# A neighbour-max graph kernel: three base rounds instead of four, rows in blocks, late rounds at two widths

## The reference

```python
h = maximum(layernorm(x), 0)
vals, idx = top_k(where(adj != 0, -arange(N), -inf), 25)
agg = max over the kept neighbours of h[idx]        # (with 0 where 25 or fewer)
out = x + relu(concat([h, agg], -1) @ W + b)
```

## Time and profile before

| | |
|---|---|
| median of 3 runs | 662.07 us (659.44 to 663.03) |
| the profiled execution's own time | 664.44 us |
| its span, first to last instruction | 661.5 us |
| TensorE busy / VectorE busy | 596.5 / 597.0 us |
| ScalarE busy / GpSimd busy | 401.7 / 96.3 us |
| DMA queue q1 | 55.6% of 16 engines |
| mean granted TensorE clock | 0.980 |

### The profile page before, as it was taken

The page is one execution under the profiler, slowest core; times in us unless marked ns, Lnnn a source line. Parts: engine busy times, 40 slices in busy tenths (PEclk is TensorE's granted clock), DMA queues, the critical chain, the costliest instruction groups (busy, mean ns, idle before and its releaser), DMA issues.

```text
span 661.5 us, 9819 instructions
## 1 busy us (share of the span) xinstructions
PE 596.5 (90%) x2800; PEld 249.8 (38%) x2800; DVE 597.0 (90%) x731; ACT 401.7 (61%) x552; POOL 96.3 (15%) x142
## 2 busy tenths in 40 slices
PE   4678979899998999999998999999998999999886
PEld 2213333343434334343433444343433434343423
DVE  4965969999998999999999999999999999999996
ACT  3346837767486756858577666858477664846210
POOL 1400005000060002400060002400060000500000
PEclk9968989999999999999999999999999999999998
DMA  8745875858259593567558485567558262231100
GB/s 342 233 116 204 322 190 205 218 158 274 55 210 231 184 241 121 193 166 250 166 206 237 146 248 174 190 160 266 149 211 237 99 184 64 91 149 34 47 16 16
DMA packets 99437, 115.79 MB, mean 175 GB/s; under 512 B 66003, under 2 KB 85718, under 8 KB 94934
## 3 DMA queue, kind: packets, MB, share of 16 engines
q1 hardware_dynamic: 98262, 114.46, 55.6%
q10 hardware_dynamic: 1152, 1.05, 0.5%
HBM read 58.85 MB, written 20.97 MB: 121 GB/s over the span
## 4 chain that ended last, share of the span: by engine, by line
PE 53%; DVE 23%; issue 10%; DMA 5%; ACT 5%; SPq 2%; DVEq 1%; ACTq 0%
PE picked L639 17%; PE picked L640 15%; PE ring L568 9%; DVE best L827 8%; DVE late_hot L839 5%; DVE best L833 4%; PE final L666 2%; PE side L597 2%; PE side L596 2%; PE final L670 2%; DMA late_skew<-late 2%; DVE hot L814 2%; PE final L620 1%; DMA kept<-chosen 1%; ACT late L480 1%
## 5 line engine op out<-in xcount | busy, mean ns | idle before, releaser
L827 DVE TENSOR_TENSOR best<-picked,best 128x1024 f32<-128x1024 f32 x224 | 270.0, 1218 | 23.3 <-PE picked L640 21.9
L639 PE MATMUL picked<-hot,h_hi 128*128 128x512 f16 x512 | 196.6, 384 | 11.9 <-DVE best L833 6.8
L640 PE MATMUL picked<-hot,h_lo 128*128 128x512 f16 x512 | 195.9, 383 | 0.0
L639 PE MATMUL picked<-late_hot,hi_skew 128*128 128x512 f16 x344 | 130.5, 379 | 19.3 <-DVE late_hot L839 10.9
L640 PE MATMUL picked<-late_hot,lo_skew 128*128 128x512 f16 x344 | 130.3, 379 | 0.0
L833 DVE TENSOR_TENSOR best<-picked,best 128x1024 f32<-128x1024 f32 x86 | 105.0, 1221 | 15.4 <-PE picked L640 14.9
L467 ACT ACTIVATE late_rank<-ring,late_bias 128x512 bf16<-128x512 f32 x128 | 81.9, 686 | 60.4 <-PE ring L568 60.1
L467 ACT ACTIVATE rank<-ring,late_bias 128x512 bf16<-128x512 f32 x120 | 82.5, 688 | 49.0 <-PE ring L568 48.8
L475 ACT ACTIVATE chosen<-side,bias_cut 128x512 bf16<-128x512 f32 x120 | 81.9, 682 | 16.7 <-PE side L597 16.7
L498 ACT COPY best<-picked 128x1024 f32<-128x1024 f32 x32 | 32.4, 1013 | 85.3 <-PE picked L640 85.3
L639 PEld LDWEIGHTS picked<-hot,h_hi 128*128 128x128 f16 x512 | 50.4, 99 | 86.0 <-DVE best L827 15.5
(11 more groups left out here) (89 smaller groups left out, 490.9 us busy)
## 6 DMA issues: line engine op xcount, KB each, us to landing
adj_in<-in_adj_dram SPq DMA_DIRECT2D x15, 2048.0 KB, 8.6
picks<-kept SPq DMA_DIRECT2D x15, 1024.0 KB, 5.0
kept<-chosen SPq DMA_DIRECT2D x112, 128.0 KB, 3.1
late_skew<-late SPq DMA_DIRECT2D x32, 192.0 KB, 4.0
x_in<-in_x_dram SPq DMA_DIRECT2D x8, 512.0 KB, 6.3
late_skew<-late SPq DMA_DIRECT2D x16, 256.0 KB, 4.8
late_skew<-late SPq DMA_DIRECT2D x32, 128.0 KB, 3.6
xres<-in_x_dram SPq DMA_DIRECT2D x16, 256.0 KB, 2.7
```

The source lines that it names most:

```text
L639: nc.tensor.matmul(dst, hi[:, slot, k, :], onehot, start=start, stop=False)
L640: return nc.tensor.matmul(dst, lo[:, slot, k, :], onehot, start=False, stop=stop)
L827: nc.vector.tensor_tensor(best[:, half, s, :, :], picked[s][:, :, :], best[:, half, s, :, :], ALU.max).then_inc(picked_read, 1)
```

## The change

BASE becomes 3: a group has 12 uses, uses 4 to 11 in its own step. Placing is spread over uses 6 to 11 and ranks over 5 to 10, 8 blocks over 6 uses each. Six blocks of late ranks, not four, stand between use 1 and `project`. Rows are laid out by blocks: row q*128 + p of a group is at column q*128 + p, where before it was row p*4 + q; the adjacency, residual and output DMAs have 4 runs per partition where they had one. The count is reduced separately for columns 0 to 255 and 256 to 511, GpSimd works out two loop counts, and the late rounds run n+1 times at 512 columns, then m times (m at least 1) at 256 columns. The gain of the next batch's normalisation is computed at the end of an even group, where it was done in use 5 of an odd group.

```diff
-BASE = 4
+BASE = 3
+    WIDE = ROWS // 2
-    SELECT_WITH, RANK_WITH = spread_over(7, 14), spread_over(6, 13)
-    LATE_EARLY, LATE_WITH, COUNT_WITH, COUNT_USE, LATE_HOT_USES = 4, {4: (4, 5), 5: (6, 7)}, (6, 7), 8, (13, 14)
-    LATE_USES, HIGH_USE, TURN_USE = {14: (0, 1), 15: (2, 3)}, 10, 15
-    STATS_USES, MOMENTS_USE, GAIN_USE = (9, 10), 12, 5
+    SELECT_WITH, RANK_WITH = spread_over(6, 11), spread_over(5, 10)
+    LATE_EARLY, LATE_WITH, COUNT_WITH, COUNT_USE, LATE_HOT_USES = 6, {4: (6, 7)}, (5, 6), 7, (8, 9)
+    LATE_USES, HIGH_USE, TURN_USE = {11: (0, 1, 2, 3)}, 8, 11
+    STATS_USES, MOMENTS_USE = (7, 8), 9
-    adj_v = adj.rearrange("b (h p q) j -> (b h) p (q j)", p=P, q=Q)
+    adj_v = adj.rearrange("b (h q p) j -> (b h) p q j", p=P, q=Q)
...
-                nc.gpsimd.tensor_scalar(late_half[:, :], late_other[:, 0:1], late_other[:, 1:2], late_other[:, 2:3], ALU.max,
-                                        ALU.max).then_inc(late_halved, 1)
...
+                for i in range(2):
+                    nc.gpsimd.tensor_scalar(late_half[:, i:i + 1], late_other[:, 0, i:i + 1], late_other[:, 1, i:i + 1], late_other[:, 2, i:i + 1],
+                                            ALU.max, ALU.max).then_inc(late_halved, 1)
+                nc.gpsimd.tensor_scalar(late_full[:, 1:2], late_half[:, 1:2], late_other[:, 3, 1:2], None, ALU.max).then_inc(late_joined, 1)
+                nc.gpsimd.tensor_scalar(late_rounds[0:1, s, 1:2], late_full[:, 1:2], 1.0, None, ALU.max).then_inc(rounds_known, 1)
+                nc.gpsimd.tensor_scalar(late_full[:, 0:1], late_half[:, 0:1], late_other[:, 3, 0:1], late_full[:, 1:2], ALU.max,
+                                        ALU.subtract).then_inc(rest_known, 1)
+                nc.gpsimd.tensor_scalar(late_rounds[0:1, s, 0:1], late_full[:, 0:1], 1.0, None, ALU.max).then_inc(rounds_known, 1)
...
+                n = pe.value_load(late_rounds[0:1, u % 2, 1:2], min_val=1, max_val=NEIGHBOURS)
+                m = pe.value_load(late_rounds[0:1, u % 2, 0:1], min_val=1, max_val=NEIGHBOURS)
                 with pe.Fori(0, n) as r:
-                    late_round(g, done, r, slot)
+                    late_round(g, done, r, slot, ROWS)
                 pe.reg_add(rounds_done, rounds_done, n)
                 done = pe.snap(rounds_done)
-                late_round(g, done, 0, slot)
+                late_round(g, done, 0, slot, ROWS)
                 pe.reg_add(rounds_done, rounds_done, 1)
+                done = pe.snap(rounds_done)
+                with pe.Fori(0, m) as r:
+                    late_round(g, done, r, slot, WIDE)
...
-                    late_ranks(g + 1, at + LATE_AT, 0)
-                    late_ranks(g + 1, at + LATE_AT, 1)
-                    pick_pair(g + 1, 2, next_slot)
-                    late_ranks(g + 1, at + LATE_AT, 2)
-                    pick_pair(g + 1, 3, next_slot)
-                    late_ranks(g + 1, at + LATE_AT, 3)
+                    for k in (0, 1):
+                        late_ranks(g + 1, at + LATE_AT, k)
+                    for use in (2, 3):
+                        pick_pair(g + 1, use, next_slot)
+                        for k in (2 * use - 2, 2 * use - 1):
+                            late_ranks(g + 1, at + LATE_AT, k)
...
                 for i in range(2):
-                    take_late(s, i, done, 0)
+                    take_late(s, i, done, 0, ROWS)
+                    make_late_hot(i, numbers[:, bass.ds(n + 2, 1)], WIDE)
                 dve.reg_add(rounds_done, rounds_done, 1)
+                done = dve.snap(rounds_done)
+                with dve.Fori(0, m) as r:
+                    for i in range(2):
+                        take_late(s, i, done, r, WIDE)
+                        make_late_hot(i, numbers[:, bass.ds(n + r + 3, 1)], WIDE)
```

More of the change, by code:

```diff
@@ L67, in build @@
     TURNED = 16 * Q
-    assert C == P and K == 8 and PER_BATCH == 2 and BASE == 4
+    assert C == P and K == 8 and PER_BATCH == 2 and BASE == 3
     LANDED = 16 * K
     OUT_OF = 64.0
-    adj_v = adj.rearrange("b (h p q) j -> (b h) p (q j)", p=P, q=Q)
-    xres_v = x.rearrange("b (h p q) c -> (b h) p (q c)", p=P, q=Q)
-    out_v = out.rearrange("b (h p q) c -> (b h) p (q c)", p=P, q=Q)
+    adj_v = adj.rearrange("b (h q p) j -> (b h) p q j", p=P, q=Q)
+    xres_v = x.rearrange("b (h q p) c -> (b h) p q c", p=P, q=Q)
+    out_v = out.rearrange("b (h q p) c -> (b h) p q c", p=P, q=Q)
     x_v = x.rearrange("b (p k) c -> b p (k c)", k=K)
@@ L125, in build @@
         late_rank = sb("late_rank", [P, K, ROWS], BF16)
[L126 to L129, removed]
+        late_most = sb("late_most", [P, 2], F32)
+        late_other = sb("late_other", [1, CHAINS, 2], F32)
+        late_half = sb("late_half", [1, 2], F32)
+        late_full = sb("late_full", [1, 2], F32)
+        late_rounds = sb("late_rounds", [P, 2, 2], I32)
         hot = sb("hot", [P, 3, K, ROWS], F16)
@@ L367, in _ @@
             nc.gpsimd.memset(eye32[:, :], 1.0).then_inc(basics_made, 1)
-            nc.gpsimd.iota(numbers_i[:, :], pattern=[[1, 32]], base=0, channel_multiplier=0).then_inc(basics_made, 1)
+            nc.gpsimd.iota(numbers_i[:, :], pattern=[[1, 64]], base=0, channel_multiplier=0).then_inc(basics_made, 1)
             nc.gpsimd.iota(late_bias_i[:, :], pattern=[[0, CHAINS], [P, LINK]], base=1, channel_multiplier=1).then_inc(basics_made, 1)
@@ L419, in fold_count @@
                 for c in range(CHAINS):
-                    nc.gpsimd.tensor_scalar(late_other[:, c:c + 1], late_most[c * PART:c * PART + 1, :], LINK * P / 2 - 1, 1.0, ALU.add,
+                    nc.gpsimd.tensor_scalar(late_other[:, c, :], late_most[c * PART:c * PART + 1, :], LINK * P / 2 - 1, 1.0, ALU.add,
                                             ALU.max).then_inc(late_folded, 1)
@@ L672, in project, with late_round @@
                 last.then_inc(final_written, 1)
-            def late_round(g, done, r, slot):
+            def late_round(g, done, r, slot, width):
                 for s in range(2):
                     pe.wait_ge(picked_read, (g + 1) * READ - 1 + s)
-                    pe.wait_ge(late_hot_made[s], done + r + 1)
+                    pe.wait_ge(late_hot_made[s], done + (r + (g + 1)))
                     pe.wait_ge(late_read[s], done + r + 1)
@@ L682, in late_round @@
                             k = s * HALF + j * LINK + i
-                            last = pick(picked[s][:, j, :], hi_skew, lo_skew, k, late_hot[:, k, :], slot, i == 0, i == LINK - 1)
+                            last = pick(picked[s][:, j, 0:width], hi_skew, lo_skew, k, late_hot[:, k, 0:width], slot, i == 0,
+                                        i == LINK - 1)
                     last.then_inc(late_written[s], 1)
@@ L828, in take_pair, with take_late, make_late_hot @@
                                         ALU.max).then_inc(picked_read, 1)
-            def take_late(s, i, done, r):
+            def take_late(s, i, done, r, width):
                 dve.wait_ge(late_written[i], done + r + 1)
-                nc.vector.tensor_tensor(best[:, s, i, :, :], picked[i][:, :, :], best[:, s, i, :, :],
+                nc.vector.tensor_tensor(best[:, s, i, :, 0:width], picked[i][:, :, 0:width], best[:, s, i, :, 0:width],
                                         ALU.max).then_inc(late_read[i], 1)
-            def make_late_hot(i, which):
+            def make_late_hot(i, which, width):
                 part = slice(i * HALF, (i + 1) * HALF)
-                nc.vector.tensor_scalar(late_hot[:, part, :], late_rank[:, part, :], which, None,
+                nc.vector.tensor_scalar(late_hot[:, part, 0:width], late_rank[:, part, 0:width], which, None,
                                         ALU.is_equal).then_inc(late_hot_made[i], 1)
@@ L923, in step @@
                     take_pair(g, use, s)
-                    if use == 5:
-                        make_hot(BASE, s)
-                    if use == GAIN_USE and more and u % PER_BATCH == PER_BATCH - 1:
-                        make_gain(batch_of(it, u + 1))
                     if use == HIGH_USE and more and u % PER_BATCH == PER_BATCH - 1:
@@ L933, in step @@
                         dve.wait_ge(ring_read, at + REST_AT + K)
-                        make_late_hot(LATE_HOT_USES.index(use), numbers[:, 1:2])
+                        make_late_hot(LATE_HOT_USES.index(use), numbers[:, 1:2], ROWS)
                     if use in STATS_USES and ahead:
@@ L968, in step @@
                     take_pair(g + 1, 3, 1 - s)
+                if ahead:
+                    make_gain(batch_of(it, u) + 1)
                 finish_group(g, s, 16 * (it * (UNROLL // 2) + u // 2 + 1))
```

53 lines of the change are left out of this document (33 added, 20 removed).

## The result

The changed kernel takes 718.42 us (median of 4 runs, 716.17 to 720.21), the kernel before 661.59 us; the ratio is 1.0857, 95% interval 1.0817 to 1.0898. Slower, as forecast, but the loss is 57 us where 34.5 were forecast, and 718.4 lies just above the range's end of 718. The profiled span is 718.0 us against 661.5.

A forecast was written before the change was run, and what follows sets the result against it. TensorE's beat was taken to bound the base part, a loop of take, late_hot and 8 matmuls the late part. Base -39, late rounds +58.5 and work behind them +15 made +34.5 on 662.07: near 697 us, range 672 to 718.

The forecast's parts named there:

- Base part: Use 4 to first late take: odd groups save 2.8 us, even 1.15, the last two 5.7 each; 39 us less.
- GpSimd's ten operations: Ten tiny operations in place of six, between use 7's count and the late rounds: covered, costing nothing; uncovered 1 to 2 us a group.
- The placing chain: Placing k waits for ScalarE's chosen k-1, 1.38 us a block; TensorE waits 3.0 us a group, mainly at uses 6 and 9.
- Rival 1: Placing waits in the base part don't bite, so it gains 83 us, not 39: 653 us, faster; chance 0.07 (fully).
- The late part: Three more full rounds at 3.86 us and 21 half rounds, 46.9 us: 58.5 us more in sum.
- Rival 3: Half-width late rounds cost nearly a full one: +34 us, 731 us; chance 0.05.
- rival 5: The row split fails and rows from 256 on need as many late rounds: 66 full ones, 727 us; chance 0.01.
- Behind the late rounds: Two more late-rank blocks, three matmuls, between use 3 and project: 1.0 us in 15 groups, 15 us more.
- Rival 2: TensorE's clock falls twice a group at use 6's wait and half-round gaps: adds 20 to 35 us, 725 us; chance 0.08.
- Rival 4: The skew comes late, each odd group waiting 1 us or more for late_skew: +10, 707 us; chance 0.07.
- The range: Whole kernel, 672 to 718 us; lower end from half the placing waits gone and half rounds at their lower bound.
- the walk through its program: TensorE's in-order base part from use 4 to use 11: 58 matmuls, two counts and 3.0 us of waits, ending at 16.36 us.

The follow-up runs named there:

- before_two_reads: The kernel before, with TensorE reading its count twice: 664.97 us, ratio 1.0046.
- read_m_later: The changed kernel, with TensorE's read of the second count m moved from in front of the full-width rounds to behind them: 706.03 us, ratio 1.0672.
- third_read: The changed kernel, with TensorE reading m twice, so three reads in front of the late rounds: 735.22 us, ratio 1.1126.
- place_8_uses: The changed kernel, with a group's eight placings spread over uses 4 to 11, one a use: 690.66 us, ratio 1.046.
- four_late_blocks_early: The changed kernel, with four blocks of late ranks in front of project and the other four at uses 4 and 5: 719.75 us, ratio 1.0884.
- four_edits: The changed kernel with placings over uses 4 to 11, m read behind full rounds, four early late-rank blocks, and use 11's placing before its picks: 679.86 us, ratio 1.0282.

## Why the prediction missed its range

- **Base part, the step that failed.** "The late rounds then start after the reading of two counts, 0.3 us (my estimate)." It is 1.5 us, 1.2 more. The estimate had no row behind it, and no bound in the sum or in the range. The kernel before has one read in the same place, and it doesn't show there in odd groups (group 7 with one read, then group 7 of before_two_reads with two):

```profile
347.63 0.38 PE L640 MATMUL picked<-hot,h_lo 128*128 128x512 f16 x1
348.63 0.38 PE L639 MATMUL picked<-late_hot,hi_skew 128*128 128x512 f16 x1 [0.62 <-DVE best L827]
...
347.61 0.38 PE L640 MATMUL picked<-hot,h_lo 128*128 128x512 f16 x1
348.61 0.38 PE L639 MATMUL picked<-late_hot,hi_skew 128*128 128x512 f16 x1 [0.61 <-DVE best L828]
```

  It is 1.00 us from start to start both times, so this gap says nothing of a read's price. read_m_later and third_read show 0.64 to 0.67 us a read. Behind placing 7 only its two matmuls (0.43 us) are queued. In group 7 this costs VectorE 1.1 us of the forecast's 2.8.
- **The size of it.** The odd groups 1 to 13 saved 1.7 us and not 2.8, 7.8 us together; the even ones 2 to 12 0.4 and not 1.15, 4.6 us; groups 14 and 15 3.3 and 2.8 and not 5.7, 5.2 us. These are the 17.6 us of the table. With one read fewer (read_m_later) the even groups save the 1.15 us forecast, but for one with 0.93, and the odd ones 2.4; the other read, 0.65 where 0.3 was allowed for both, is what the odd ones still lack. So the reads are the miss in these groups. Further 2.4 us are missing before take 4 of group 1 (0.9 of them in a late stage of 13.37 us for 12.45, with a granted clock of 0.61 from 80 to 84 us) and 2.3 in the late stage (half of them the fallen clock of group 15); the stage behind gives 0.9 back, and 0.5 lies behind VectorE's last instruction. Together that is the 22 us. In group 14 the 2.4 us missing are 0.7 for the second read (14.53 in read_m_later for 15.21), 1.05 for fold_count's further operations, and 0.65 that no run separates, the price of the first read.
- **GpSimd's ten operations.** Costed at nothing. Right in the groups that place (17.95 us with ten and 17.97 with six); in groups 14 and 15, without the placing's 3 us, fold_count with its 4.6 us ends last. The price I set without cover, 1 to 2 us a group, fits the 1.05 us of group 14.
- **The placing chain.** Right in mechanism, place and size, to 0.1 us at each of four points; place_8_uses wins 28 us by taking most of these waits away. Rival 1 is refuted.
- **The late part.** Right. The 58.5 us forecast are net of the shorter last take (16 x 0.53), which falls behind the late stage, and hold group 0; for the late stage of groups 1 to 15 alone they make 64.4, and 66.7 were measured. A half round is 2.26 (2.25). Rival 3 (a half round near a full one's 3.95) falls by that, rival 5 by the counts.
- **Behind the late rounds.** 9.37 us against 8.90 - 0.53 + 1.0. four_late_blocks_early shows the 1.0 and that moving it back wins nothing. The 0.68 us of rows 7 is idle time of the weight loads, though; the matmuls lose 0.36 us at such a wait. There are two in group 7 now (starts 391.05, 391.62 and 392.20, 0.57 us apart where matmuls in a row are 0.215), and one more of them with the three matmuls' 0.65 makes the 1.0.
- **Rival 2, the clock.** Not in the middle groups of the changed kernel: 0.989 against 0.980 before, with falls in the opening (60 to 64 and 80 to 84 us, 0.57 and 0.61) and in group 15. third_read, with 0.65 us more idle time in each gap, has it at 0.964. The Trainium skill's sentence that activity releases the throttle (TensorE: Matmul & The Clock Gate, What's actually happening) agrees with both. The gap of 1.5 us in the middle groups left the clock at 1.00 from 141 to 684 us.
- **Rival 4, the skew.** It costs nothing in the changed kernel: the stage behind the late rounds is 9.37 or 9.38 us in all of groups 1 to 14, where before groups 3 and 7 had 9.36 and 9.47 in place of 8.90, with waits of 0.65 and 0.76 us for late_skew.
- **The range.** Its lower end doesn't follow from its two conditions: half of the placing waits (14 x 1.5 = 21 us) and half rounds at their lower bound (12 us) give 664, not 672. Its upper end, 718, was worked out from no bound of a term.
- **The balance.** With the four edits 680 us is left against 662, so waits of the new hand order aren't the whole loss. A base round costs VectorE 5.7 us and TensorE 3.4; it was replaced by 0.2 full and 1.3 half rounds a group, 3.7 us on the path. The claim that what the base part can give back stops where TensorE's ranks, placings and counts, which didn't shrink, bind is an argument from the walk through its program; no run isolates it, and whether another hand order would win the 18 us was not tried.

## What to carry to other kernels

Before a loop with a computed count, ask what is queued on the engine that reads it: here a read of 0.65 us was free behind four queued matmuls (four_edits) and cost in full behind two. When iterations are taken out, walk the in-order program once with everything that stays: a serial chain (here 1.38 us a block over two engines) that was hidden at one block a use comes out at once where two blocks meet. And count data-dependent iterations from the inputs: the counts came out exactly, and the largest term of the sum with them. And give an estimate that has no row a bound of its own: the figure that failed here had neither, and was five times too small.

## What wasn't expected of the hardware

A late_hot of 0.74 us took 2.60 us while GpSimd ran a subtraction over two tensors (195.58 to 197.70) and ended only after it. The Trainium skill (SBUF — State Buffer, Terms) says that VectorE and GpSimd arbitrate for one port pair, exclusive and held for a whole instruction, so that the loser blocks; the trace agrees for this pair. In the kernel before late_hot too ends 0.5 us after the subtraction, and in place_8_uses a make_hot that meets its end takes 1.75 us in place of 1.22 (354.36). The takes aren't slowed: in group 1 of the changed kernel one lies wholly inside the same subtraction and lasts 1.23 us as ever (GpSimd, then VectorE):

```profile
118.99 2.12 POOL L386 TENSOR_TENSOR h_lo<-h,h_hi 128x1024 f16<-128x1024 f32 x1
119.84 1.23 DVE L849 TENSOR_TENSOR best<-picked,best 128x1024 f32<-128x1024 f32 x1 [0.29 <-PE picked L656]
```

And a register read of a count holds TensorE's program for 0.64 to 0.67 us.
